# Perceiver-style network on one Trainium2 core: half of the next attention's inputs made beside the experts' second sweep, and outputs two items behind

## What is computed

```python
x = x + ffn(layernorm(x))       # router picks 6 of 32 experts per token
                                # expert: silu(x @ gate.T) * (x @ up.T) @ down.T, one shared expert
x = x + xattn(layernorm(x), ctx, ctx)
# Q = layernorm(x) @ W_Q + b_Q ; K = ctx @ W_K + b_K ; V = ctx @ W_V + b_V
# 16 heads of 8 channels; softmax(Q K^T / sqrt(8)) V @ W_O + b_O ; ctx: 32 items x 1601 tokens x 128
```

## Time and profile before

| | us |
|---|---|
| median of three runs | 1929.55 |
| lowest, highest | 1923.28, 1940.96 |
| the profiled execution, whole | 1934.74 |
| its span | 1933.0 |
| PE, DVE, ACT, POOL busy | 1753.6, 1398.0, 1242.7, 576.6 |

### The profile page before, as it was taken

The page is one execution under the profiler, slowest core; times in us unless marked ns, Lnnn a source line. Parts: engine busy times, 40 slices in busy tenths (PEclk is TensorE's granted clock), DMA queues, the critical chain, the costliest instruction groups (busy, mean ns, idle before and its releaser), DMA issues. The chain is left out here.

```text
span 1933.0 us, 68149 instructions
## 1 busy us (share of the span) xinstructions
PE 1753.6 (91%) x29700; PEld 1106.4 (57%) x29720; DVE 1398.0 (72%) x2412; ACT 1242.7 (64%) x2173; POOL 576.6 (30%) x463
## 2 busy tenths in 40 slices
PE   7899999999989587899779999999999999847898
PEld 5577777777765264434436665666665665535443
DVE  2677777777753675578478988988988997356565
ACT  3377777777743381222248888888888888447243
POOL 4322232232130441456312222222222220033365
PEclk8899999999999688899779999999999999868899
DMA  4355555555400300456465655655555652030011
GB/s 156 95 142 138 149 145 144 149 141 144 116 4 0 66 4 17 120 153 174 92 109 104 104 97 105 103 97 105 102 99 105 103 98 28 1 68 4 28 42 41
DMA packets 66556, 178.40 MB, mean 92 GB/s; under 512 B 20276, under 2 KB 24500, under 8 KB 65844
## 3 DMA queue, kind: packets, MB, share of 16 engines
q1 hardware_dynamic: 64436, 170.85, 40.0%
q10 hardware_dynamic: 1824, 3.20, 0.8%
HBM read 84.39 MB, written 1.31 MB: 44 GB/s over the span
## 5 line engine op out<-in xcount | busy, mean ns | idle before, releaser
L648 ACT ACTIVATE Pb<-ps 128x512 f32<-128x512 f32 (+1 forms) x832 | 451.9, 597 | 50.4 <-PE ps L595 31.8
L615 PE MATMUL ps<-Pb,V 128*17 128x64 f32 (+1 forms) x13312 | 380.6, 248 | 0.7 <-ACT Pb L648 0.7
L724 DVE TENSOR_REDUCE MX<-ps 128x2 f32<-128x804 f32 (+1 forms) x385 | 364.0, 984 | 18.7 <-PE ps L561 17.5
L615 PEld LDWEIGHTS ps<-Pb,V 128*17 128x17 f32 (+1 forms) x13312 | 250.6, 97 | 87.2 <-issue 43.5
L726 DVE TENSOR_REDUCE MX<-ps 128x1 f32<-128x402 f32 (+1 forms) x512 | 265.9, 569 | 30.8 <-PE ps L565 24.8
L768 POOL TENSOR_TENSOR ABO<-CT 128x1601 bf16<-128x1601 f32 x44 | 125.9, 2863 | 538.7 <-DMA CT<-ctxT 538.7
L651 ACT ACTIVATE Pb<-ps 128x1024 f32<-128x1024 f32 (+1 forms) x224 | 204.6, 959 | 40.9 <-PE ps L599 38.3
L561 PE MATMUL ps<-KST,QW 50*128 50x402 bf16 (+1 forms) x1024 | 177.9, 343 | 13.1 <-DVE MX L724 5.6
L595 PE MATMUL ps<-QW,KST 50*128 50x128 bf16 (+1 forms) x3328 | 165.4, 219 | 4.3 <-ACT Pb L648 2.4
L671 ACT ACTIVATE V<-ps 128x512 f32<-128x512 f32 (+1 forms) x256 | 129.3, 521 | 48.3 <-PE ps L547 39.8
L565 PE MATMUL ps<-KST,QW 96*128 96x402 bf16 (+1 forms) x512 | 148.0, 338 | 6.4 <-POOL QW L758 0.4
(11 more groups left out here) (261 smaller groups left out, 3228.4 us busy)
## 6 DMA issues: line engine op xcount, KB each, us to landing
CT<-ctxT SPq DMA_DIRECT2D x44, 800.5 KB, 4.7
KST<-HL SPq DMA_DIRECT2D x320, 100.1 KB, 3.0
KST<-C SPq DMA_DIRECT2D x320, 100.1 KB, 3.0
Pb<-routed SPq DMA_DIRECT2D x64, 256.0 KB, 3.9
ABO<-ctxT SPq DMA_DIRECT2D x10, 800.5 KB, 4.9
T<-ctxT SPq DMA_DIRECT2D x10, 800.5 KB, 4.4
KST<-HL SPq DMA_DIRECT2D x128, 50.0 KB, 2.7
KST<-C SPq DMA_DIRECT2D x128, 50.0 KB, 2.7
```

Source lines behind the costliest of these rows:

```text
L615: mm = nc.tensor.matmul(ps[32 * quad:32 * quad + m, SUM, oc:oc + nh * S], V[0:n, b % 2, tile, v0:v0 + m], Pb[0:n, buffer(b, x), ti * att.W ...
L648: nc.scalar.activation(Pb[0:n, buffer(b, x), i * 512:(i + 1) * 512], score_bank(b, x, i)[0:n, :], ACT.Exp, scale=att.scale).then_inc(exps, 1)
L724: nc.vector.reduce_max(MX[:, b % 2, 2 * j:2 * j + 2], work(job)[:, :, 0:n], AX.X).then_inc(freed["dve"], 1)
```

## The change

Three parts.

1. **Outputs two items behind.** TensorE's queue pairs `up(item)` with `down(item - 2)`, across the two sweeps without a drain. Hidden values get three buffers in place of two (HID, HLO, now in ABO and no longer in QW). `up` waits for the first multiply of the item before (`mid`) and no longer for the second. `sp_experts` and `sp_weights` keep their waits. The expert loads go on across the sweeps in one list. VectorE adds sweep one's result to the stream after item 1 of sweep two.
2. **Beside sweep two** (`next_attention`): after item 3 centring, after 4 variance, after 5 spreading of the norm, for chunks 0 and 1 (those of sweep one, so half the tokens), in banks 6 and 7; after 6 the queries of these chunks; after 7 to 14 their stacking, two DMAs per item from ScalarE's queue; after 8 and 9 the keys of the attention's item 0, after 11 and 12 its values; from 11 to 16 the stacking of these keys, three DMAs per item from SyncE's queue. Its context is loaded into QW ahead of the experts.
3. **The rest of norm and queries** (chunks 2 and 3) and the keys of item 1 stand between item 0's sixteen maxima, by a table `PROLOGUE`. The late queries are stacked by SyncE after item 1's keys; context 3 is loaded first and no longer last.

```diff
+PROLOGUE = [(t[0], int(t[1:])) for t in (
+    "M0 a2 M1 a3 M2 b2 M3 b3 M4 c2 M5 c3 M6 d2 M7 d3 M8 v0 M9 K0 H0 M10 K1 H1 M11 K2 H2 M12 K3 H3 M13 w0 M14 M15 R0").split()]
...
-            HID = [Pb[:, 1, :], spare[:, 0:4 * CH].bitcast(F32)]
-            HLO = [spare[:, (2 + u) * 2 * CH:(3 + u) * 2 * CH] for u in range(2)]
+            HID = [Pb[:, 1, :], ABO[:, 0:2 * CH], ABO[:, 2 * CH:4 * CH]]
+            HLO = [ABO[:, (4 + u) * CH:(5 + u) * CH].bitcast(BF16) for u in range(3)]
...
-                    eng.wait_ge(s["hid"], unit(sweep, item, cc) - 1)
+                    eng.wait_ge(*multiplied(sweep, item - 1, cc) if item else multiplied(sweep - 1, NI - 1, cc))
...
+                for i, (sweep, item) in enumerate(items):
+                    for cc in range(2):
+                        up(sweep, item, cc)
+                        if i >= 2:
+                            down(*items[i - 2], cc)
...
+                    if sweep:
+                        beside(item)
...
+                for i, (sweep, item) in enumerate(routed):
+                    sp_weights(sweep, item)
+                    if SLOTS <= i + 2 < len(routed):
+                        sp_experts(*routed[i + 2])
+                    if sweep:
+                        beside(item)
...
+        def next_attention(role, eng, item):
...
+            norm = {3: "centre", 4: "variance", 5: "spread"}.get(item)
+            if item == 1:
+                split_weights(role, eng, XA1, 1)
+            if norm is not None:
+                for c in range(2):
+                    layernorm(role, eng, 6, X, T, (sem("moe_out"), 1), step=norm, c=c, bank=bank)
+            if item == 6:
+                project_split(role, eng, 1, w("xa1_q"), "bq1", (sem("ln_out"), 6 * NC + 1), HLQ, bank, (0, 1))
+            if item == 4 and role == "pool":
+                cross_attention(role, eng, XA1, "early", "bo1", step=("L", 0))
+            if item in (8, 9) and role != "sp":
+                for j in (2 * item - 16, 2 * item - 15):
+                    cross_attention(role, eng, XA1, "early", "bo1", step=("K", j))
+            if item in (11, 12) and role != "sp":
+                for j in (2 * item - 22, 2 * item - 21):
+                    cross_attention(role, eng, XA1, "early", "bo1", step=("V", j))
+            if item in range(7, 15) and role == "act":
+                if item == 7:
+                    eng.wait_ge(sem("proj_lo"), NC + 2)
+                stack_queries(eng, "halves_early", 0, 2 * (item - 7), 2 * (item - 6))
+            if item in range(11, 17) and role == "sp":
+                cross_attention(role, eng, XA1, "early", "bo1", step=("S", 3 * (item - 11)))
...
             if role == "sp":
+                if att.early:
+                    sp_context(3)
                 sp_context(2)
                 sp_stack(1)
-                sp_context(3)
+                if att.early:
+                    eng.wait_ge(sem("proj_lo"), 2 * NC)
+                    stack_queries(eng, "halves_late", 2, 0, 16)
+                else:
+                    sp_context(3)
```

More of the change, by code:

```diff
@@ L87, in __init__ @@
         self.halved = heads == 16
+        self.early = cross and heads == 16
         self.parts = 2 if self.halved else 1
@@ L403, in split_halves, with stack_queries, project_split @@
             return stacked_s, (call + 1) * 16 * 16
-        def project_split(role, eng, call, weights, bname, ready, parts, bank=lo_bank):
+        def stack_queries(eng, name, first, begin, end):
+            cols = slice(first * CH, (first + 2) * CH)
+            for i, (g, h, part) in enumerate((g, h, part) for g in range(4) for h in range(2) for part in range(2)):
+                row, c0 = 64 * h, 32 * g + 16 * h
+                if begin <= i < end:
+                    if part == 0:
+                        eng.dma_start(QS[row:row + 32, g, cols],
+                                      HLQ[c0:c0 + 16, 0:1, cols].broadcast_to([16, 2, 2 * CH])).then_inc(sem(name), 16)
+                    else:
+                        eng.dma_start(QS[row + 34:row + 50, g, cols], HLQ[c0:c0 + 16, 1, cols]).then_inc(sem(name), 16)
+        def project_split(role, eng, call, weights, bname, ready, parts, bank=lo_bank, chunks=range(NC)):
             pe_s, hi_s, lo_s = sem("proj_sum"), sem("proj_hi"), sem("proj_lo")
             n = call * NC
-            for c in range(NC):
+            for c in chunks:
                 if role == "pe":
@@ L604, in pe_product @@
                 if x == 0:
-                    eng.wait_ge(*emptied((b, "V", 3), "act"))
+                    if att.early and b == 0:
+                        eng.wait_ge(early_act, 8)
+                    else:
+                        eng.wait_ge(*emptied((b, "V", 3), "act"))
                     if b:
@@ L1595, in dve_item, with dve_add @@
                     ins.then_inc(s["hid"], 1)
+            def dve_add(sweep):
+                for cc in range(2):
+                    eng.wait_ge(s["down"], unit(sweep, NI - 1, cc) + 1)
+                    x = ck(X, 2 * sweep + cc)
+                    nc.vector.tensor_tensor(x, x, ps[:, cc, :], ALU.add).then_inc(s["out"], 1)
             def sp_experts(sweep, item):
```

354 lines of the change are left out of this document (246 added, 108 removed).

## The result

Median 1926.5 us (20 runs) against 1931.5 us for the kernel before (20 runs). The ratio over all runs is 0.9971, 95% interval [0.9959, 0.9984], that is 5.6 us less [3.1, 7.9]; the two medians alone lie 5.0 us apart. A second measurement (12 runs) gave 0.9963 [0.9944, 0.9981], 7.1 us less [3.7, 10.8]. The forecast was 11 us less: 1918.5 us, from a median of three runs of 1929.55.

A forecast was written before the change was run, and what follows sets the result against it. TensorE nearly fills the second expert sweep, with much room from the experts to the next attention's first scores. Experts +19 us and the path behind them -29.9 give -11: 1918.5 us from 1929.55, range 1902 to 1932.

The forecast's parts named there:

- The mechanism: Expert sweeps: routing weights queue behind an expert load awaiting later outputs; three slots take at least 13.7 us, 4.57 each.
- Rival A: Expert sweeps: SyncE's order does not bind, TensorE runs slots back to back; experts end 4 us later, 1903.7 us; chance 26%.
- The experts: Both expert sweeps together: they end 3.8 + 15.2 = 19 us later, bounds +13 to +25.
- 5.5 each: Sweep two, slots 13 to 16: SyncE's three key-stacking issues per item lengthen the loop to some 5.5 us a slot.
- The list: Behind the experts, last output to item 1's first maximum: shorter by 29.9 us, bounds -27 to -32.
- 31.0 against 60.9: Time in us from the last expert output to item 1's first maximum, after the change against before it.
- some 2 us of waits: Start of the work behind the experts: VectorE waits some 2 us for ScalarE, beside 24.0 us of its own work.
- Item 1's wait for stacked keys: Behind the experts: item 1's first maximum waits for stacked keys, 3 us after VectorE has finished its work there.
- Item 2's keys: Second cross attention: stacked some 7 us late, landing at about 51 us, wanted at 54; costs nothing, 3 us margin.
- ScalarE at nothing: Sweep two: ScalarE's added table switches, squares, evictions and sixteen DMA issues fit its idle 2.9 us per item, costing nothing.
- Rival B: Behind the experts: at granted 0.5 to 0.57 5 us more pass, item 2's late keys cost 3; 1926.5 us; chance 9%.
- Rival C: Expert sweeps: waits bring TensorE down to 1.2 GHz, 3.1 us more per such slot; ten give 1949.5 us; chance 6%.

The follow-up runs named there:

- the second experiment: Kernel before with only outputs two items behind, plus each expert's load one place later in SyncE's queue: ratio 1.0007 [0.9984, 1.0030] to the kernel before; experts 147.3 us.

## Why the forecast gain was too high

**The mechanism: shown.** SyncE issues expert and pair back to back, VectorE waits for the pair, TensorE for GpSimd's weights, and slots are 4.57 us, to the hundredth as forecast. The hundredths are luck: the sum took 4.4 us for the second transfer of a pair to land, the median is 4.2 in this kernel, and with that it gives 4.5. That SyncE's place in the order is the cause, and not the deeper pipeline itself, the second experiment shows. Rival A (the order does not bind) is out. Its number, 1903.7, was the change with this cost removed; removed by outputs one behind, it measured 1912.7 (1932.9 for the kernel before in the same series).

**The experts: +19 forecast, +20.0 and +20.5 measured.** By its steps: the end of item 3's slot in sweep two came 3.8 and 4.3 us later than before (3.8 forecast). The next nine slots, in which the work stands beside, took 46.2 and 46.4 us (46.6 forecast, from 884.24 to 930.41 in the first execution), four of them some 5.65 us long with TensorE working throughout:

```profile
884.04 1.88 PE L304 MATMUL ps<-X,W 128*128 128x512 f32 x4
...
889.68 1.84 PE L312 MATMUL ps<-W,C 128*128 128x1 f32 x16
...
895.31 1.95 PE L285 MATMUL ps<-W,COL 128*128 128x128 f32 x16
...
901.02 1.88 PE L445 MATMUL ps<-T,W 128*128 128x512 f32 x4
```

The rest, with the stacking, took 26.9 and 26.6 for 25.6 forecast. Slots 13 and 14 together took 11.3 and 10.7 us for 11.0, each with the routing pair behind three issues, as the first of them shows (930.41 to 936.70). What is 1 us and more short is the end: from slot 14 to the last output 15.7 and 16.0 us, for 14.5 ("5.5 each", and 3.5), with TensorE waiting 2.07 and 1.51 us in one place for VectorE's first multiply.

```profile
930.41 0.33 SPq L1793 DMA_DIRECT2D CT<-experts  x1
930.79 0.54 SPq L883 DMA_DIRECT2D KST<-HL  x1
...
932.83 1.25 SPq L1805 DMA_DIRECT2D Pb<-routed  x2
936.70 0.33 SPq L1793 DMA_DIRECT2D CT<-experts  x1
```

**The list: -29.9 forecast, -27.3 measured. This is the step that failed,** "31.0 against 60.9". Two executions of each kernel give 60.9 and 58.0 before, 32.9 and 31.4 after; means 59.5 and 32.2. The base was one execution in which the norm happened to run partly at the lower clock, and that put 1.5 us too much into it.

The other 1.2 us are in the list after, and the traces name the term. The forecast had VectorE set the pace, with "some 2 us of waits", and item 1's keys done 22.7 us after the last output. They are done after 25.7 and 24.2 us. VectorE has worked 20.0 and 19.8 us by then, about as counted, but has been idle 5.7 and 4.4 us: in the first twelve microseconds it is TensorE that is busy all but throughout (12.0 and 11.9), at a granted 0.72 and 0.86 in the two executions, and VectorE waits for its steps and ScalarE's. From the keys to item 1's first maximum it is 7.2 us in both, for 7.5 forecast. So the term that failed is the waiting between engines, 2 us and 0.8 for the half clock allowed, 4.4 to 5.7 measured.

The experts' part was 1.2 us short, the list's 2.6. With +20.2 and -27.3 the sum is -7.1, the stage's own mean is -7.2 (222.8 for 230.0), and the ratios say -5.6 and -7.1, with intervals that both hold 7. Nothing is left over that can be told from noise.

**Item 1's wait for stacked keys: seen, and a real part of the list.** 2.79 and 2.63 us, as forecast (3). Earlier keys removed the wait and gave no time, but not because it is worth nothing: the keys came only 2 to 5 us sooner, and small VectorE instructions that ran into GpSimd's low parts became the last thing waited for. Item 2's keys, stacked late too, cost nothing, as forecast: ScalarE copies its shift rows 20.6 us after item 1's in both kernels (1013.35 and 1033.96 us here, 1015.29 and 1035.90 before). The forecast took the copy at 992.22 for item 1's; it is item 0's, but the distance of 23 us to the next, on which it relied, stands.

**ScalarE at nothing: held.** In sweep two TensorE is busy 44.68 of 45 us. The table load beside the experts shows 1.28 us and the next activation 0.01 us behind it, in the changed kernel's ScalarE rows:

```profile
889.83 1.28 ACT L325 ACT_TABLE_LOAD   x1
891.12 0.26 ACT L325 ACTIVATE DEV<-ps,epst 128x4 f32<-128x4 f32 x1
```

The Trainium skill (*ScalarE: Activation LUTs*, What ACT_TABLE_LOAD costs) adds a drain, for 2.66 us in all; no run here shows it.

**Rival B** (the list not that short) points the right way and was too large for the changed kernel: 32.9 and 31.4 us for the list in place of 31.0, where B had 36. But the two kernels with the stacking last, at a granted 0.50 in the first twelve microseconds, had 35.9: the price that B named, at the clock that it named. **Rival C** (the clock falls among the experts) did not come true in the changed kernel: the granted clock is 1.00 from 800 to 958 us, with waits of 0.92 us in sweep one and of up to 2.07 us late in sweep two. The Trainium skill (*TensorE: Matmul & The Clock Gate*, A second HAM failure mode) tells of a kernel in which frequent short idles make the clock go to and fro; this trace shows no such thing. After one wait of 2.24 us in another kernel the clock was down for 3.4 us.

**What was missed altogether** is a question the forecast did not ask: what each half of the change is worth. Work beside the experts with outputs one behind gives 21 us. The other half, outputs two behind, takes 11 us of it away in the stage (222.8 for 211.7) and 14 to 15 by the ratios, with some 6 us to either side; the changed kernel keeps 6 to 7.

## What to carry to other kernels

A queue's order is written for a pipeline's depth. When work is put one stage further back, every wait in the queues that counts it moves with it, and what stands behind that wait is late; look there first, and change depth and queue together or neither. A span read from one execution contains the clock that it happened to get: before a difference is built on a stretch where the granted clock is between its levels, take the same stretch from a second execution. And when an edit removes a wait and no time is gained, look at what is waited for in its place, down to single instructions: here it was a small one that took 2.8 us in place of 0.17 beside a GpSimd instruction that had begun before it.

## What the runs showed that was not expected

- Two executions of the same instructions differ by 11.4 us in the first 780 us, and by 1.1 us in the 222 us behind it. All kernels here had their store between 778.65 and 790.06. The same experts took 167.1 to 170.3 us in four executions.
- After a wait of 2.24 us TensorE was granted 0.51 for 3.4 us in one kernel, and after one of 2.25 us at the same place 1.00 in another.
- With the wait ahead of the list filled, the clock was 1.00 for six microseconds and 0.72 in the next six, in which TensorE was never idle; the changed kernel's second execution had the same values without the filling. Being busy did not keep it up there.
- VectorE's small instructions on the maxima (128x8, from SBUF) were held up by GpSimd. In the four kernels with outputs two behind alone or keys early they took up to 2.84 us in place of 0.17, each while a GpSimd instruction (of 2.86 us, or 1.04) ran that had begun before, and each ended within 0.1 us of its end. In the kernel before the GpSimd instruction began 0.13 us after the two were over. The rest of that kernel shows the same: of its 192 such instructions (they write MH), 24 took 0.57 to 1.04 us, all 24 beside a GpSimd instruction that had begun before them, and all ended within 0.04 us of its end; the other 168 took 0.17 or 0.18. The maxima from PSUM, beside the same GpSimd instructions, kept their 0.98 us (977.21 in the changed kernel).
- With the stacking moved behind the last pair, both executions (outputs two and one behind) had the list at 35.9 us, and the granted clock at 0.50 in twelve of its first fourteen microseconds. That is open: a shift of a few microseconds in when the list starts, or the transfers that ran beside it (DMA share 0.90 in the five microseconds behind the last output, for 0.63 in the changed kernel), may be what matters, and no run separates the two.
